# Graph network of four layers: in the relational layer, edges into the first 128 nodes by counts times resident rows

## What is computed

```python
def _L1_gnn_ref(x, edge_index, edge_type, weight, bias):
    row, col = (edge_index[0], edge_index[1])          # row = src, col = dst
    xt = jnp.einsum('ni,rio->rno', x, weight)          # 8 types x 6250 rows of 256
    messages = xt[edge_type, col]
    out = jax.ops.segment_sum(messages, row, num_segments=num_nodes)
    return jax.nn.relu(out + bias)
...
x = x + _L0_gnn_ref(h, edge_attr_3, src, dst, ...)     # edge MLP, sums by dst
x = x + _L1_gnn_ref(h, edge_index, edge_type_8, ...)   # relational, sums by src
x = x + _L2_gnn_ref(h, edge_index, ...)                # attention, sums by dst
x = x + _L3_gnn_ref(h, edge_index, ...)                # graph convolution, sums by src
```

## Time and profile before

| | us |
|---|---|
| median of 3 runs | 5305.56 |
| lowest, highest | 5305.24, 5307.98 |
| the profiled execution: first to last instruction (its span; no time around it is recorded) | 6597.1 |
| relational pass, first to last gather, in the profiled execution | 3098.9 to 4278.2 |
| last pass, first to last gather | 5720.2 to 6569.7 |

### The profile page before, as it was taken

How to read it: one execution, slowest core, us unless ns; L and a number is a source line. 1 busy time by engine, 2 the same in 40 slices (tenths; PEclk the granted TensorE clock), 3 DMA queues, 4 the chain that set the end, 5 groups by cost and what they waited for, 6 DMA issues and landing times. The chain is left out here.

```text
span 6597.1 us, 65618 instructions
## 1 busy us (share of the span) xinstructions
PE 3895.4 (59%) x14913; PEld 2594.0 (39%) x14914; DVE 2562.6 (39%) x8644; ACT 1792.3 (27%) x5648; POOL 3799.2 (58%) x3942
## 2 busy tenths in 40 slices
PE   4232666667641533596455555566777777577777
PEld 2121333333320510242333333355566555455555
DVE  4223444444430300132222222255555555644443
ACT  0111555555530400011000000044444444400000
POOL 3554666666666077402666666666666666277776
PEclk7565666766665765796676666667777777688888
DMA  1011332332310010144433333323333333233332
GB/s 48 20 41 60 88 88 87 89 89 87 88 45 3 0 42 22 59 148 141 124 99 98 98 98 98 96 82 87 87 87 86 87 86 89 77 98 99 99 98 87
DMA packets 277662, 527.83 MB, mean 80 GB/s; under 512 B 80566, under 2 KB 175259, under 8 KB 277049
## 3 DMA queue, kind: packets, MB, share of 16 engines
q0 software_dynamic: 176144, 422.24, 22.5%
q1 hardware_dynamic: 85200, 86.14, 3.9%
q10 hardware_dynamic: 15960, 15.41, 0.7%
HBM read 433.63 MB, written 89.82 MB: 79 GB/s over the span
## 5 line engine op out<-in xcount | busy, mean ns | idle before, releaser
L675 POOL DMA_INDIRECT got_attend_src_dst<-dram_gtab,gather_src x832 | 800.4, 962 | 531.0 <-DVE msg_attend_src_dst L747 320.9
L577 POOL DMA_INDIRECT dram_rec_src<-rec_src x784 | 766.5, 978 | 509.6 <-issue 243.5
L1760 POOL DMA_INDIRECT got_edge_mlp_src_dst<-dram_ptab,gather_src x832 | 786.3, 945 | 463.2 <-DVE pre_edge_mlp_src_dst L1802 252.9
L1591 POOL DMA_INDIRECT got_rgcn<-dram_xtab,gather_of_type x831 | 788.3, 949 | 392.5 <-issue 187.9
L1886 PE MATMUL psS_edge_mlp_src_dst<-msg_edge_mlp_src_dst,hot_edge_mlp_src_dst 128*128 128x256 f32 x1664 | 736.1, 568 | 434.0 <-DVE sage_sums L1783 223.6
L1591 POOL DMA_INDIRECT got_gcn<-dram_htab,gather_rest x586 | 616.5, 1052 | 234.1 <-issue 148.9
L861 PE MATMUL psS_attend_src_dst<-msg_attend_src_dst,hot_attend_src_dst 128*128 128x264 f32 x1664 | 700.8, 513 | 19.5 <-DVE msg_attend_src_dst L747 14.3
L2091 PE MATMUL psO_tab<-w_tab,hT_tab 128*128 128x512 f32 (+1 forms) x980 | 474.4, 633 | 350.1 <-issue 200.5
L1886 PEld LDWEIGHTS psS_edge_mlp_src_dst<-msg_edge_mlp_src_dst,hot_edge_mlp_src_dst 128*128 128x128 f32 x1664 | 388.5, 269 | 589.7 <-issue 338.8
L1682 PE MATMUL psS_rgcn<-got_rgcn,hot_rgcn 128*128 128x257 f32 x1662 | 543.8, 471 | 79.7 <-DMA got_rgcn<-dram_xtab,gather_of_type 55.0
L1783 DVE TENSOR_TENSOR sage_sums<-sage_sums,psS_edge_mlp_src_dst 128x256 f32 x832 | 347.8, 418 | 523.6 <-PE psS_edge_mlp_src_dst L1886 246.1
(11 more groups left out here) (397 smaller groups left out, 5878.7 us busy)
## 6 DMA issues: line engine op xcount, KB each, us to landing
dram_xtab<-out_tab SPq DMA_DIRECT2D x48, 1024.0 KB
got_edge_mlp_src_dst<-dram_ptab,gather_src POOLq DMA_INDIRECT x832
got_attend_src_dst<-dram_gtab,gather_src POOLq DMA_INDIRECT x832
got_rgcn<-dram_xtab,gather_of_type POOLq DMA_INDIRECT x831
dram_rec_src<-rec_src POOLq DMA_INDIRECT x784
got_gcn<-dram_htab,gather_rest POOLq DMA_INDIRECT x586
dram_gtab<-sums ACTq DMA_DIRECT2D x48, 132.0 KB
x_sb<-x_in SPq DMA_DIRECT2D x1, 6144.0 KB
```

Source lines behind the costliest of these rows:

```text
L577: nc.gpsimd.indirect_dma_start(edges.to, bass.IndirectOffsetOnAxis(edges.rec[:, column, PLACE:PLACE + 1].bitcast(I32), 0), edges.rec[:, co ...
L675: nc.gpsimd.indirect_dma_start(got[:, t % U, 0:w], None, table, bass.IndirectOffsetOnAxis(row_of[:, t:t + 1], 0)).then_inc(row_in[t % U], 16)
L1591: nc.gpsimd.indirect_dma_start(got[:, t % U, 0:D], None, table, bass.IndirectOffsetOnAxis(row_of[:, t:t + 1], 0)).then_inc(row_in[t % U], 16)
L1760: nc.gpsimd.indirect_dma_start(got[:, t % U, 0:width], None, table, bass.IndirectOffsetOnAxis(row_of[:, t:t + 1], 0)).then_inc(row_in[t % ...
```

## The change

In the relational pass, edges with dst below 128 are no longer gathered. A new layout `most` (15 tiles per bucket, 733 in all, 6 chunks) holds the others; the first 3 tiles of `near` hold those below 128. For each of these 3 tiles ScalarE makes the one-hots, with Abs of the difference and Relu of one minus it: the source place (128 wide) and type and destination together (8 x 128 = 1024 wide). `near_sum` then has 8 blocks x 3 tiles of bf16 matmuls, `near_product` 8 blocks with 257 columns, over the first 128 rows of each of the 8 parts of `xtab`, which stay in SBUF. In this pass one-hots and counts have one buffer each. Counted from the inputs, a bucket has at most 333 edges below 128 (room for 384) and 1844 others (room for 1920); the last one has 250 and 1468 (room for 384 and 1590).

The split counts for both limits; the order stage behind it has 14 chunks in place of 8, and the three `near` chunks turn two lists; the order stage of `whole` turns one list in place of two. The lists of `whole` are freed afterwards. The last pass keeps its form, with its two one-hots in one tile. The bank psR of the pass's end is shared with psT.

```diff
+MOST, FIRST = 15, 3
...
 split_stage:
-            link(nc.vector.tensor_scalar(low[:, :], c.gather["dst"][:, 0:whole.n], float(P * DEEP), None, ALU.is_lt))
-            link(nc.vector.scalar_tensor_tensor(mine[:, :], c.rel["whole"][:, 0:whole.n], float(P), low[:, :], ALU.is_lt, ALU.mult))
+            for q, limit in enumerate((P * DEEP, P)):
+                link(nc.vector.tensor_scalar(low[:, q, :], c.gather["dst"][:, 0:whole.n], float(limit), None, ALU.is_lt))
+                link(nc.vector.scalar_tensor_tensor(mine[:, q, :], ...))
+                nc.vector.tensor_reduce(few[:, q, 0:NB - 1], ...)
...
+def first_near(c):
+    rows = c.xtab.rearrange("(r n) d -> n r d", r=NREL)[0:P, :, :]
+    return Near(c.near_type, [[c.sh.N, NREL], [1, P]], NREL, FIRST, D + 1, rows, True, 1)
+
+def last_near(c):
+    rows = c.htab[0:DEEP * P, :].rearrange("(k p) d -> p k d", p=P)
+    return Near(c.near_dst, [[1, DEEP * P]], DEEP, NEAR, D, rows, False, 2)
...
 bucket_pass, ScalarE:
             def times_of(b):
                 act.wait_ge(near_sums, b + 1)
-                wait_count(act, near_made, b - 1)
+                wait_count(act, near_made, b + 1 - bufs)
...
+            def near_gap(b, i):
+                t, n = listed[b] + i, made_by[b] + i
+                wait_count(act, near_hots, n - 1)
+                nc.scalar.activation(apart[:, n % 2, 0:P], c.iota[:, :], ACT.Abs, bias=to[:, t:t + 1], scale=-1.0)
+                nc.scalar.activation(apart[:, n % 2, P:], wide[:, :], ACT.Abs, bias=of[:, t:t + 1], scale=-1.0).then_inc(near_gaps, 1)
+
+            def near_hot(b, i):
+                n = made_by[b] + i
+                wait_count(act, near_sums, b + 1 - bufs)
+                act.wait_ge(near_gaps, n + 1)
+                nc.scalar.activation(hot_near[:, b % bufs, i, :], apart[:, n % 2, :], ACT.Relu, bias=c.ones[:, 0:1],
+                                     scale=-1.0).then_inc(near_hots, 1)
...
             for t, (b, k) in enumerate(where):
+                near_gap(b + 1, k - 2)
+                near_hot(b + 1, k - 3)
                 if near is not None and k == 3:
                     times_of(b)
...
 bucket_pass, TensorE:
-                for a in range(DEEP):
-                    last = nc.tensor.matmul(psS[b % 2][:, 0:D], times[:, b % 2, a, :], rows[:, a, :], ...)
+                for a in range(deep):
+                    last = nc.tensor.matmul(psS[b % 2][:, 0:near.cols], times[:, b % bufs, a, :], rows[:, a, :], ...)
...
-        stage(nc, bucket_pass, c, "rgcn", c.xtab, c.gather["of_type"], c.rel["whole"], c.layouts["whole"], RgcnBehind)
+            stage(nc, bucket_pass, c, "rgcn", c.xtab, c.gather["most"], c.rel["most"], c.layouts["most"], RgcnBehind, first_near(c))
```

More of the change, by code:

```diff
@@ L1247, in _ @@
+            link(nc.vector.tensor_tensor(late[0:NB, 5:6], c.counts["src"][0:NB, :], count[0:NB, 2:3], ALU.subtract))
+            nc.vector.tensor_tensor(late[0:NB, 2:3], late[0:NB, 4:5], room["rest"][0:NB, :], ALU.is_gt)
+            nc.vector.tensor_tensor(late[0:NB, 3:4], late[0:NB, 5:6], room["most"][0:NB, :], ALU.is_gt).then_inc(begun, 1)
             dve.wait_ge(laid, 1)
             dve.wait_ge(numbered, 1)
-            for x in ("rest", "near"):
+            for x in lists:
                 k = c.layouts[x].chunks
@@ L1261, in _ @@
         def _(pe):
-            pe.wait_ge(fewer, 1)
-            nc.tensor.matmul(ps[0:NB, 0:1], few[:, 0:NB], c.ones[:, 0:1], start=True, stop=True).then_inc(counted, 1)
+            pe.wait_ge(fewer, 2)
+            for q in range(2):
+                last = nc.tensor.matmul(ps[0:NB, q:q + 1], few[:, q, 0:NB], c.ones[:, 0:1], start=True, stop=True)
+            last.then_inc(counted, 1)
             pe.wait_ge(begun, 1)
[L1265 to L1268, removed]
+            for x in lists:
+                pe.wait_ge(roomy[x], 5)
+            nc.tensor.matmul(ps[0:1, 8:12], c.ones[0:NB, 0:1], late[0:NB, 0:4], start=True, stop=True)
+            for x in lists:
                 for k in range(c.layouts[x].chunks):
@@ L1556, in bucket_pass @@
         if near is not None:
-            to, of, rows_d = near
+            to, of, deep = c.rel["near"], near.of, near.deep
             layn = c.layouts["near"]
[L1559 to L1562, removed]
+            listed = [sum(layn.counts[0:b]) for b in range(NB)]
+            tiles_of = [min(near.tiles, n) for n in layn.counts]
+            made_by = [sum(tiles_of[0:b]) for b in range(NB + 1)]
+            wide = sb("wide", [P, deep * P])
+            bufs = near.bufs
+            hot_near = sb("hot_near", [P, bufs, near.tiles, P + deep * P], BF16)
+            apart, near_gaps = sb("apart", [P, 2, P + deep * P], BF16) if near.on_act else None, sem("near_gaps")
+            times, rows = sb("times", [P, bufs, deep, P]), sb("rows", [P, deep, near.cols])
             psA = [[pt(f"psA{q}{h}") for h in range(2)] for q in range(2)]
@@ L1574, in _ @@
             if near is not None:
-                sp.dma_start(rows[:, :, :], rows_d[0:DEEP * P, :].rearrange("(k p) d -> p k d", p=P)).then_inc(rows_in, 16)
+                sp.dma_start(rows[:, :, 0:D], near.rows).then_inc(rows_in, 16)
                 sp.wait_ge(rows_in, 16)
@@ L1672, in near_product @@
                     pe.wait_ge(rows_in, 16)
-                for a in range(DEEP):
-                    last = nc.tensor.matmul(psS[b % 2][:, 0:D], times[:, b % 2, a, :], rows[:, a, :], start=False, stop=False, skip_group_check=True)
+                    if near.cols > D:
+                        pe.wait_ge(widened, 1)
+                for a in range(deep):
+                    last = nc.tensor.matmul(psS[b % 2][:, 0:near.cols], times[:, b % bufs, a, :], rows[:, a, :], start=False, stop=False, skip_group_check=True)
                 last.then_inc(near_made, 1)
```

142 lines of the change are left out of this document (87 added, 55 removed).

## The result

The changed kernel takes 5270.7 us (median of 4 runs, 5269.84 to 5271.56), the kernel before beside it on the same chip 5306.25 (5305.24 to 5307.98): a ratio of 0.9931, 95% interval 0.9917 to 0.9945, so 35.5 us faster. The prediction was 5350, slower. Its range of 5222 to 5440 held the time, because it reached far into the faster rival's; the sign was wrong.

A forecast was written before the change was run, and what follows sets the result against it. Gathers bound the kernel before; after, a TensorE, VectorE and ScalarE ring sets the relational pass. (20.0 - 19.5) x 49 = +24, plus 20 for stages: 5305.56 + 44 = 5350 us, range 5222 to 5440.

The forecast's parts named there:

- the faster rival: Relational pass: gathers stay the bound because the ring fits under GpSimd's 17.2 us; 5214, or 5243 at 18.2; chance 0.30.
- from the profile to a run: Gathers: recorded 1.25 us each cannot hold in a run; 1.145 taken, so 19.5 us per bucket before the change.
- the 950 us of other work: Recorded span outside gathering: of 6597.1 us, 5647.5 is gathering and 950 other work, kept whole or shrunk by 0.804.
- the profiled execution: Relational pass as recorded, with 2.9 us of pauses per bucket: 22.9 against 24.1, span near 6558.
- The ring: Relational pass: loop through TensorE, VectorE and ScalarE sets the bucket, 18.2 us at full clock, 20.0 with slow clock; 0.50.
- S: Start of a bucket's first tile in the relational pass, from which h was counted: done 9.5 us later.
- the gathers stay the bound: Relational pass: ring within GpSimd's 17.2 us, pass loses 112, whole 5214; or 5243 with ring at 18.2; chance 0.30.
- ScalarE's prices: ScalarE, relational pass: gap 1.40 and one-hot 1.19, 2.6 us per tile; with counts and old work 10.5 a bucket.
- The clock: TensorE after its 5.4 us wait runs at half clock for 3.4 to 5 us: 1.8 us added per bucket.
- The stages: Work around the relational pass: split and masks 7, chunk reads 7.5, start of pass 5 to 6; +20, between 10 and 28.

The follow-up runs named there:

- the second recording: The kernel before the change, unedited, recorded once more for a profile: one run, 5313.44 us.
- the earlier trace: The profile of the kernel before the change that the prediction was made from: span 6597.1 us, against a median of 5305.56.
- experiment 1: The kernel before the change, recorded again with no edit: one run, 5313.44 us.
- the first recording: The profile of the unedited kernel before the change that the prediction read: span 6597.1 us, against a median of 5305.56.
- experiment 2: Changed kernel with ScalarE's near gaps and one-hots of the next bucket moved behind h (k = 2 to 5 became 7 to 10): 5196.61 us.
- experiment 3: Changed kernel without the near part of the relational pass, so edges with dst below 128 are missing from the second layer: 5195.97 us.
- experiment 4: Changed kernel with only 4 of the 8 near products in the relational pass, so four types miss their near edges: 5199.54 us.
- experiment 7: Changed kernel with 64 unread bf16 matmuls on TensorE, placed in its wait before the transposes: 5205.55 us.
- experiment 5: Changed kernel with ScalarE's h at k = 5 in place of k = 4, behind one more gap and one-hot: 5269.35 us.
- experiment 6: Changed kernel with h at k = 5 and one more Relu of 1152 elements into a spare tile ahead of the third one-hot: 5350.86 us.
- experiment 8: Changed kernel with the relational pass's near one-hots made by VectorE in place of ScalarE: 5228.02 us.
- experiment 10: Changed kernel with the relational pass's near work on ScalarE behind h, and the last pass's one-hots on ScalarE too, started 2 tiles in: 5130.98 us.

## Why the prediction was wrong

**The step that failed: from the profile to a run.** I wrote that the recorded 1.25 us "cannot hold in a run: 3887 x 1.25 + 764 is 5623" and took 1.145. It does hold, in this pass in every kernel in which gathers are the bound (18.78 to 18.80 for 15). The 5623 was wrong in its other part: I let the 950 us of other work in the recording shrink by no more than the whole, by 0.804. By the same count the second recording has 3769.6 us busy and 1248.3 idle before them, of which 40.3 stage borders, so, with 27.5 for the orders, 5005 us of gathering (1.29 a gather over all stages, 1.254 in this pass) and 307 of other work: the 950 had shrunk by 0.32. Half of the recording's excess of 1285 us (5647.5 - 5005 = 642) lay between gathers, the other half (643) in stretches without them. The instructions of GpSimd, VectorE and ScalarE kept their durations (the earlier trace rows and experiment 1: 303.3, 74.9 and 788.2 us in the pass for VectorE, ScalarE and GpSimd, against 308.0, 74.9 and 788.2); waits had grown. The largest growth of one group's waits stood before the reads of `order_whole`, first in the first recording, then in the second:

```profile
L1135 POOL DMA_INDIRECT rows_order_whole<-dram_rec_src,off_whole x7 | 6.6, 946 | 321.8 <-SPq L1117 320.0 <-issue 1.8
```

```profile
L1135 POOL DMA_INDIRECT rows_order_whole<-dram_rec_src,off_whole x7 | 6.6, 945 | 12.8 <-SPq L1117 11.0 <-issue 1.8
```

Proportional shrinking was an assumption with no row behind it, whereas the 1.25 had every row.

**What it cost.** Bucket before 21.3 us, predicted 19.5: 1.8 x 49 = 88 us, more than the 79 us between forecast and result. With 21.3 the forecast's own sum is (20.0 - 21.3) x 49 + 20 = -44, so 5262, 9 below the result. I had also worked out the profiled execution at 22.9 against 24.1, that is 1.2 less per bucket; the measured difference is (1040.5 - 986.9) / 49 = 1.1. The comparison inside one execution was right, the step out of it spoiled it.

**The ring: right in kind, its size in part by luck.** h ended 9.0 us after S (said 9.5), TensorE stood 4.84 (5.4), the bucket was 20.48 in the steady part and 20.2 over the pass (20.0). Experiments 2, 3, 4 and 7 each break the ring at another place and each gives 18.8. But the two terms of the sum were off in opposite directions: the ring at full clock is 17.6 us (said 18.2, experiment 7), and the clock adds 2.9 (said 1.8). And experiment 5, in which h comes 1.14 us later, gives the same 20.48, so a sum of terms does not fix this length. The rival "the gathers stay the bound" had the direction only; its condition, a ring with slack, wasn't met. Whoever asks what the change could have given: 98 x 1.25 = 122 us of gathers, of which experiment 2 has all in the pass (1040.5 - 916.5 = 124) and the change less than half.

**ScalarE's prices: right.** Groups of the changed kernel by shape, xcount | busy, mean ns:

```profile
L1700 ACT ACTIVATE hot_near_rgcn<-apart_rgcn,ones 128x1152 bf16<-128x1152 bf16 x147 | 182.6, 1243 | 2.9 <-PE psA_rgcn L1732 2.9
L1691 ACT ACTIVATE apart_rgcn<-wide_rgcn,near_type 128x1024 bf16<-128x1024 f32 x147 | 166.8, 1135 | 0.0
L1681 ACT COPY times_rgcn<-psA_rgcn 128x512 f32<-128x512 f32 x98 | 51.2, 571 | 0.0
```

I had 1.265 and 1.156 for the first two; both are 2% high.

**The clock: right in kind, but its price is no constant.** I added 1.8 us per bucket for slow MATMULs. The products alone lost 5.92 - 3.64 = 2.3, the whole bucket 20.48 - 17.6 = 2.9, and experiment 7 takes it away. The granted clock is 0.83 over the pass with the wait in it, against 0.99 with filler in the wait. In the changed kernel the distances between VectorE's sums run 22.11, 20.33, 20.40, 20.44, 20.46, 20.47, 20.47, 20.48 and stay at 20.48; in experiment 5 they come from the other side, 20.87, 20.68, 20.58, 20.53, 20.51, to the same 20.48. From the second distance on the deviation halves from bucket to bucket. My reading is that the rise of the clock comes at moments that the bucket does not set: a bucket that begins d later then has d less at 0.50 before the rise and ends only d/2 later, and a wait longer by 1.14 us moves the transposes by 2.3 against the rise and loses 1.14 less to the clock. The traces show a shift of that size. In windows laid inside the slow stretches, first of the changed kernel, then of experiment 5, then two neighbouring ones of experiment 6, the last number but two is the granted clock:

```profile
2823.60:2830.20 6.60, 5.87 (x15) 4.76 (x16) 0.29 (x1) 2.08 (x4) 5.08 (x6) 0.50 0.40 112
```

```profile
2820.00:2826.70 6.70, 3.55 (x10) 2.90 (x11) 0.28 (x1) 3.47 (x5) 5.18 (x6) 0.50 0.38 112
```

```profile
2801.00:2807.60 6.60, 3.53 (x10) 2.89 (x11) 0.30 (x1) 3.39 (x5) 5.08 (x6) 0.50 0.38 108
...
2821.40:2831.50 10.10, 5.80 (x15) 4.70 (x16) 0.32 (x1) 4.62 (x6) 6.30 (x7) 0.50 0.35 105
```

The clock rises 6.0 us after the transposes begin in the changed kernel (2824.34 to 2830.3; the window 2830.00:2830.40 reads 0.64) and 3.6 after them in experiment 5 (2823.15 to 2826.8; 2826.40:2826.90 reads 0.61): the slow stretch itself stays 6.8 us long, but 3.2 us of it in place of 0.9 fall into the wait, where TensorE has nothing to multiply. In experiment 6 it lasts 6.8 us in one bucket and 10.2 in the next, and the rise comes 3.6 and 5.9 us after the transposes: these are the buckets with 4.78 and with 5.89 us of products. So the two distances of experiment 6 come from the clock. What sets its moments no run here shows; that they are not the bucket's is a reading that fits all three kernels.

**The stages: a term a little large.** Predicted were +20, of which 15.5 up to the first gather (7 for the split, 7.5 for the reads, 1 for the 1024 numbers); up to there +14.6 were measured. The other 4 to 5 us, for the first one-hots, do not show: VectorE's first sum comes 21.6 us after the first gather, 2.8 more than 15 x 1.254, and before the change it came 24.3 after, 3.0 more than 17 x 1.254.

## What to carry to other kernels

When a recording is longer than the runs, compare kernels inside the recording and carry over the difference; here the instruction durations (TensorE's apart) and the start-to-start spacings of an engine that wasn't waiting (1.25 us a gather in both recordings) were a run's, the waits were not. When work moves to an engine that stands in a loop with the bound one, write down that engine's queue in order and count from the loop's first event to the value that the others stand for: its total (484 of 1010 us here) didn't show the loss, its position did (74 us for two changed numbers). And when moving work between engines, look at the mean duration of instructions on the engines that weren't touched (GpSimd's gathers here, 990 ns in place of 948).

## What the runs showed of the hardware

An indirect gather of 128 rows of 1 KB takes 0.95 us of GpSimd and the next starts 0.30 us later, 1.25 us in all, on the stretches shown where nothing holds it. Its duration went with what VectorE did beside it. In the relational pass it is 948 ns on average with no bf16 one-hots on VectorE and 990 with three tiles of them a bucket of 15; in the last pass it is 1054 with six a bucket of 12, and 951 to 953 when ScalarE makes those six. It is the gathers that run beside such a one-hot of VectorE that are longer, 1.27 us on average against 0.95 for the others in the last pass, 1.14 against 0.95 in the relational pass of experiment 8. The one-hots on ScalarE are bf16 too, and the gathers stay at 948 (experiment 2) and 951 ns (experiment 10) with them. VectorE's float32 one-hots of 128 columns run beside gathers in both of these passes; in the kernel before, where the relational pass has no others, its gathers take 949 ns. Whether the bf16 output or the width of 640 and 1024 makes the difference wasn't tried.

A loop with a wait in it took a delay of 1.14 us a bucket at no cost and paid 80 us for the next such delay, since only with the first did the clock's slow stretch slide into the wait by enough to make up for it (3.2 us of 6.8 in place of 0.9; with the second it was again 3.2 of 6.8 in one bucket and 4.3 of 10.2 in the next). Matmuls whose result nobody reads, put into the wait, gave 65 us at a granted clock of 0.99 in place of 0.83.

One recording was 24% longer than another of the same kernel (6597.1 against 5311.7 us) with the instructions of three engines at the same durations (VectorE, ScalarE and GpSimd: 303.3, 74.9 and 788.2 us in the relational pass against 308.0, 74.9 and 788.2). TensorE's busy time in the pass was even lower there, 634 us against 796; why, no run here shows.
